# A shifted-window attention block on one core: a second tile for the high and low halves of q and k, an exponential moved ahead of v's evacuation, and the value projection split over two rounds

## The reference, cut to what matters

```python
y   = roll(layernorm(x), (-3, -3))
win = windows_of_7_by_7(y)                    # 2048 windows of 49 tokens
q, k, v = win @ qkv_w.T
attn = softmax(q @ k.T * 8 ** -0.5 + bias + mask)
x   = x + roll(back(attn @ v @ proj_w.T + proj_b), (3, 3))
out = x + gelu(layernorm(x) @ fc1_w.T + fc1_b) @ fc2_w.T + fc2_b
```

## Time and profile before

| what | value |
|---|---|
| median of three runs | 2187.03 us |
| the profiled execution's own time | 2188.17 us |
| its span, first to last instruction | 2186.4 us |
| TensorE matmul busy / weight loads busy | 2115.9 us (97%) / 1670.1 us (76%) |
| VectorE / ScalarE / GpSimd busy | 1681.2 (77%) / 1535.7 (70%) / 1682.9 us (77%) |
| mean granted TensorE clock | 0.996 |

### The profile page before, as it was taken

One profiled execution on the slowest core, in us unless ns is written; L12 is line 12 of the kernel. 1 busy time (PEld: TensorE's weight loads), 2 busy tenths in 40 slices (PEclk: granted clock), 3 DMA queues, 4 the chain that ended last, 5 costly groups with the idle time before them and its releaser, 6 DMA issues.

```text
span 2186.4 us, 147908 instructions
## 1 busy us (share of the span) xinstructions
PE 2115.9 (97%) x62790; PEld 1670.1 (76%) x62790; DVE 1681.2 (77%) x2975; ACT 1535.7 (70%) x2435; POOL 1682.9 (77%) x1689
## 2 busy tenths in 40 slices
PE   6999999999999999999999999999999999999997
PEld 3777777777777777777777777777777777777775
DVE  5778778777877777787777778778777877877774
ACT  4676776776777677677767777776776777677675
POOL 5777777777778777777778777777777777777774
PEclk8999999999999999999999999999999999999999
DMA  4223233232322233333232233333223232333321
GB/s 111 71 75 80 75 77 77 75 78 75 78 76 75 77 77 77 76 76 77 74 78 76 73 77 77 77 77 77 75 75 78 76 75 76 77 75 76 78 69 35
DMA packets 178588, 165.87 MB, mean 76 GB/s; under 512 B 21144, under 2 KB 152458, under 8 KB 178074
## 3 DMA queue, kind: packets, MB, share of 16 engines
q1 hardware_dynamic: 178074, 157.60, 28.5%
HBM read 28.99 MB, written 25.77 MB: 25 GB/s over the span
## 4 chain that ended last, share of the span: by engine, by line
PE 74%; SPq 9%; issue 5%; DVE 5%; ACT 3%; DMA 3%; POOL 1%; DVEq 0%; ACTq 0%; POOLq 0%
PE O L751 12%; PE S L715 9%; SPq L270 8%; PE ST L731 8%; PE M L824 8%; PE M L759 8%; PE ST L737 7%; PE M L846 7%; PE M L809 5%; PE M L791 4%; PE M L777 3%; DMA kp<-hl 3%; PE M L854 2%; DVE nm L579 2%; PE S L719 2%
## 5 line engine op out<-in xcount | busy, mean ns | idle before, releaser
L324 POOL TENSOR_TENSOR nmd<-diag,nm 121x392 f16<-121x392 f16 x1024 | 852.8, 840 | 452.6 <-DVE nm L579 438.3
L579 DVE TENSOR_REDUCE nm<-S 121x8 f16<-121x392 f32 x1024 | 574.7, 561 | 126.1 <-PE S L715 69.2
L424 ACT ACTIVATE pT<-ST 113x392 f32<-113x392 f32 x1024 | 481.9, 496 | 246.2 <-PE ST L737 241.3
L751 PEld LDWEIGHTS O<-vx,pT 113*49 113x49 f32 x16384 | 546.9, 126 | 45.6 <-issue 5.2
L751 PE MATMUL O<-vx,pT 113*49 113x18 f32 x16384 | 521.7, 196 | 3.9 <-issue 3.8
L715 PE MATMUL S<-kp,qp 128*49 128x49 f16 x16384 | 396.9, 186 | 20.6 <-issue 7.4
L731 PE MATMUL ST<-qp,kp 128*49 128x49 f16 x16384 | 389.7, 185 | 16.6 <-ACT pT L424 11.2
L715 PEld LDWEIGHTS S<-kp,qp 128*49 128x49 f16 x16384 | 313.2, 103 | 111.0 <-issue 63.6
L737 PE MATMUL ST<-nmd,shiftw 121*49 121x392 f16 x2048 | 349.1, 336 | 0.3 <-POOL nmd L324 0.2
L731 PEld LDWEIGHTS ST<-qp,kp 128*49 128x49 f16 x16384 | 317.9, 103 | 37.3 <-ACT pT L424 16.9
L405 ACT ACTIVATE hl<-M 128x784 f16<-128x784 f32 x128 | 105.4, 823 | 331.5 <-DMA kp<-hl 173.8
(11 more groups left out here) (90 smaller groups left out, 3258.9 us busy)
## 6 DMA issues: line engine op xcount, KB each, us to landing
qp<-hl SPq DMA_DIRECT2D x1024, 49.0 KB
kp<-hl SPq DMA_DIRECT2D x1024, 49.0 KB
xin<-in_x SPq DMA_DIRECT2D x256, 98.0 KB
out<-res SPq DMA_DIRECT2D x256, 98.0 KB
kp<-in_c_keys SPq DMA_DIRECT2D x4, 588.0 KB, 7.2
weights<-in_c_weights SPq DMA_DIRECT2D x1, 448.0 KB, 3.8
bias_t<-spread SPq DMA_DIRECT2D x2, 73.5 KB, 2.2
shiftw<-in_c_shift SPq DMA_DIRECT2D x1, 139.0 KB
```

What stands on the lines that cost most here:

```text
L324: nc.gpsimd.tensor_tensor(nmd[j % LAG][:], diag[:], nm[j % LAG][:].unsqueeze(2).broadcast_to([RM, 2 * 4, N]), ALU.mult).then_inc(s_nmd, 1)
L424: nc.scalar.activation(pT[j % LAG][:].rearrange("k w h q -> k (w h q)"), ST[0:R, j % 2, 0:HK], ACT.Exp).then_inc(s_e, 1)
L579: V.tensor_reduce(nm[j % LAG][:], S[0:RM, 0:HK].rearrange("q (h n) -> q h n", n=N), AX_X, ALU.max, negate=True).then_inc(s_nm, 1)
L751: mm = MM(O[W0 * w:W0 * w + N, (4 * p + hp) * VC:(4 * p + hp + 1) * VC], pT[j % LAG][:, w, hp, :], vx[r % RING][:, window + 2 * w, hp, :], ...
```

## The change

The change has three parts.

1. There are two `hl` tiles in place of one; unit u uses tile u mod 2. `high_parts` of unit u therefore waits for the DMAs of unit u - 2 in place of those of unit u - 1.
2. On ScalarE, in round 1, exp 7 stands ahead of `place_v` in place of behind it.
3. `project_v` is cut into two halves of 16 matmuls, one in round 1 and one in round 2, each after the transposed scores of that round. Only the second half signals `place_v`.

```diff
-        hl = sb("hl", [128, 2, 2, 2, T // 2], F16)
+        hl = [sb(f"hl{n}", [128, 2, 2, 2, T // 2], F16) for n in range(2)]
...
-                        part = hl[C * qk:C * qk + C, s, b].rearrange("m a t -> m (a t)")
+                        part = hl[r % 2][C * qk:C * qk + C, s, b].rearrange("m a t -> m (a t)")
...
             def high_parts(u, r):
                 act.wait_ge(s_qk, u + 1)
-                if later(u):
+                if later(u, 2):
                     for b in range(2):
-                        act.wait_ge(s_q[(r + 1) % 2][b], 64 * u + 64 - 64 * ((r + 1) % 2))
-                nc.scalar.activation(hl[:, 0].rearrange("m b a t -> m a b t"),
+                        act.wait_ge(s_q[r % 2][b], 64 * u - 64 * (r % 2))
+                nc.scalar.activation(hl[r % 2][:, 0].rearrange("m b a t -> m a b t"),
...
-                    if k == 1 and on_chip(a):
-                        place_v(a, m + 1)
                     u, j = at_unit(i, k, 2)
                     if on_chip(u):
                         exp(u, j)
+                    if k == 1 and on_chip(a):
+                        place_v(a, m + 1)
...
-            def project_v(u):
-                for s in range(8):
+            def project_v(u, half):
+                for s in range(4 * half, 4 * half + 4):
                     for e in range(2):
                         mm = MM(M[W0 * e:W0 * e + N, 2, C * s:C * s + C], yT[:, N * s:N * s + N], wv[:, e, :],
                                 start=True, stop=True, tile_position=(0, W0 * e))
-                mm.then_inc(s_vp, 1)
+                if half == 1:
+                    mm.then_inc(s_vp, 1)
...
-                    if k == 1 and on_chip(a):
-                        project_v(a)
+                    if k in (1, 2) and on_chip(a):
+                        project_v(a, k - 1)
```

More of the change, by code:

```diff
@@ L566, in evac_yT, with low_parts @@
                                 M[:, 1, :].rearrange("c (p w n) -> c p w n", w=2, n=W0)[:, :, :, 0:N], n1w[:, 0:1], n1b[:, 0:1], ALU.mult, ALU.add).then_inc(s_yT, 1)
-            def low_parts(u):
+            def low_parts(u, r):
                 dve.wait_ge(s_hi, u + 1)
-                V.tensor_tensor(hl[:, 1].rearrange("m b a t -> m a b t"),
+                V.tensor_tensor(hl[r % 2][:, 1].rearrange("m b a t -> m a b t"),
                                 M[:, 0:2, 0:HT].rearrange("m a (b t) -> m a b t", b=2),
-                                hl[:, 0].rearrange("m b a t -> m a b t"), ALU.subtract).then_inc(s_lo, 1)
+                                hl[r % 2][:, 0].rearrange("m b a t -> m a b t"), ALU.subtract).then_inc(s_lo, 1)
             def neg_max(u, j):
@@ L655, in body @@
                     if k == 1 and on_chip(a):
-                        low_parts(a)
+                        low_parts(a, m + 1)
                     if k == 2 and on_chip(d):
```

## The result

The changed kernel takes 2246.68 us, the median of four runs (2245.46 to 2249.72). Its ratio to the kernel before is 1.0274 (95% interval 1.026 to 1.0288), so it is 2.7% slower. I had forecast 2219 us, 1.5% slower, and a range that ends at 2245. The direction was right and the size was not. The profiled execution's span is 2245.8 us against 2186.4, which is 59 us more where I had 32. One execution behind this document stands far out: of the eight of E11, a later experiment, one took 10652.71 us for a reason that no trace shows, and without it E11's median would be 2176.97 us in place of 2177.72.

What follows compares the result with a forecast made beforehand. TensorE's list was taken to bound the kernel, with ScalarE's almost without slack in rounds 1 to 4. +68 us for the new wait, -30, -2 and -4 gave +32, or 2219 us for the median, range 2190 to 2245.

Steps and rivals of the forecast that it cites:

- Rival A: Round 4, faster: the late place_v does not reach turn_o, so only gains stay, 2145 us; chance 0.11.
- Rival B: No net change: a delay of 0.29 us at turn_o cancels 36 us of relief, 2183 to 2191 us; chance 0.05.
- rival C: Slower by the whole new wait: DMAs hold the scores, or turn_y delays evacuation and neg_max 5; 2255 us; chance 0.10.
- step 5: Round 4 on TensorE: turn_o starts 0.05 us after the second gelu, 1321.56 in place of 1320.97, 0.59 later.
- the choice of 0.55 us: Delay per pass taken at turn_o, between 0.46 and 0.59 us; over 124 passes 68 us (57 to 73).
- step 4: ScalarE behind place_v: one exp in place of two gives 0.39 us back, so table load and gelus come 0.68 later.
- my own worked value: Delay of turn_o worked out for one clean pass, 0.59 us; with scores 2 earlier it would be 0.46.
- the relief: Hold-ups gone: 30 us for the second hl tile, 2 at the start, 4 for small ones in rounds 2 to 4.

Runs made afterwards that it cites:

- E11: Kernel before with two hl tiles, and project_v cut into two halves that both stand in round 1: 2177.72 us, ratio 0.997.
- E8: Changed kernel with GELU replaced by Identity, so without the two table loads (timing only): 2161.69 us, ratio 0.9901.
- E9: Changed kernel with project_v cut into 24 matmuls in round 1 and 8 in round 2: 2232.38 us, ratio 1.0211.
- E10: Changed kernel with project_v cut into 8 matmuls in round 1 and 24 in round 2: 2269.16 us, ratio 1.0377.
- E6: Changed kernel with turn_o's two waits exchanged, second gelu first and normalise second: 2240.04 us, ratio 1.0249.
- E3: Changed kernel with the one hl tile of before, keeping exp 7 ahead of place_v and the split project_v: 2244.54 us, ratio 1.0271.
- E2: Kernel before with two hl tiles and exp 7 ahead of place_v, project_v whole: 2189.36 us, ratio 1.0012.
- E12: Kernel before with exp 7 ahead of place_v and nothing else: 2190.52 us, ratio 1.0022.
- E5: Kernel before with two hl tiles and turn_o's two waits exchanged, second gelu first and normalise second: 2179.85 us, ratio 0.9976.
- E7: Kernel before with two hl tiles and GELU replaced by Identity, so without the two table loads (timing only): 2172.74 us, ratio 0.9947.

## Why the prediction was wrong in size

**What held.** ScalarE idles ahead of `place_v` (0.60 us in the clean pass, where I had 1316.73 - 1316.16 = 0.57). `place_v` starts 2.64 us behind scores 1, where I had 1316.73 - 1314.10 = 2.63. Scores 2 come 1.52 behind scores 1, as worked out, scores 3 hardly move (2.94 in place of 2.98), the second gelu sets `turn_o`, and no wait of `high_parts` for the DMAs is left. E8 to E10 show that this is the whole cost of the split. Rival A is excluded: `turn_o` was reached. Rival B is too, since the delay at `turn_o` is 0.70 and not 0.29 us. The mechanisms of rival C don't show. TensorE's scores wait once for a DMA out of `hl`, 0.6 us. VectorE's evacuation does wait longer for `turn_y` (28.9 us in place of 5.9), but the scores' waits for `neg_max` didn't grow with it (5.9 us in place of 6.9).

**The step that failed: step 5, and the choice of 0.55 us.** I had the second gelu 0.68 us later in step 4, and the rows give nearly that: it ends 1355.97 - 1348.54 = 7.43 us behind scores 1 where it was 1320.83 - 1314.10 = 6.73, so 0.70 later. Then I let `turn_o` follow it by 0.05 us, the gap between exp 7 and its transposed scores, and so took the 0.14 us in the row of before for 0.09 us of slack. It was no slack. In the kernel before `turn_o` starts 0.14 us behind the second gelu in 78 of the 112 passes, never less, and in 105 of the 112 of the changed one. E6 shows that the 0.09 belongs to the order of the waits. The delay therefore passes in full, 0.70 us. I also went below my own worked value toward a pass in which scores 2 come earlier, and few do (15 of 112). The pass of the fourth kind grew by a little less, 0.64, so the mean clean pass grew by 0.69, from 16.30 to 16.99: 0.55 x 124 = 68 us stood for 0.69 x 124 = 85 us. This is 17 of the 27 us by which I was short.

**The other term: the relief.** I counted 30 us for the second `hl` and 6 us for the start and other hold-ups. The mean pass was 0.32 us above a clean one before. Now a clean pass is about (3 x 16.87 + 17.33) / 4 = 16.99 us, where 17.33 is the usual length of the fourth kind, and the mean is 0.11 above it. That is 0.21 us a pass, or 26 us in all, against 36 forecast, and not for my reason. E1 gives the second tile 11 us by itself, and E3 gives it nothing in the changed kernel. The rest is that the idle stretches at `place_v` and `turn_o` swallow whatever else is late: the changed kernel's 112 passes still hold 60 stops, 27 us together, and are only 13 us longer than clean ones. My count took all of ScalarE's lateness for TensorE's, and gave the single `hl` three quarters of hold-ups of which over half (21 of 36 us) are the stops. The 11 us of E1 are about a third of the 30 that I had read from ScalarE's waits.

The two terms together give 85 - 26 = 59 us, as much as the spans differ by, against the forecast's 68 - 36 = 32.

**A smaller error.** I wrote that the exchange alone costs nothing. With `project_v` whole it costs 0.15 us a clean pass (E2, E12), because exp 7 can't start before shift 7. With the split it starts where I had it, 1.56 us behind scores 1.

**What comes out of it.** Of the versions run with the reference's own function, E1, the second `hl` tile alone, is the fastest: 2174.91 us, 0.9951 of the kernel before (0.9933 to 0.9968). The intervals of E5 and E11, which have the same tile, overlap with it.

## What to carry to other kernels

Follow each engine's list from the signal that a change moves to the next place where the bound engine waits for it. An engine at 70%, as ScalarE was here, can have no slack there, and then a delay arrives whole: 0.13 and 0.22 us at v's signal became 0.14 and 0.22 at `turn_o`. Before a gap between a signal and its waiter is called slack, look for its smallest value over all passes. If many passes share it, it can be the cost of the wait, as it was here: 78 of the 112 passes of the kernel before shared 0.14 us and none had less. And what a side engine waits is not what the bound engine loses: read the bound engine's own waits for it (here 11 us where the side engine had 30), and sort the passes by how late it is.

## What the runs showed of the hardware that I had not expected

At `turn_o` the wait that stands second in the code took longer to pass than the one that stands first. From the end of the second gelu to the first matmul of `turn_o` it was 0.14 us where that wait was second (105 of the 112 passes of the changed kernel) and 0.05 to 0.06 us where it was first (101 of the 112 of E6). From the end of `normalise` it was 0.05 to 0.10 us where that wait was first (E7) and 0.15 us where it was second (E5).

In these traces the wait written second is an instruction of its own, of 51 ns, and the line of the wait written first (L797 in the changed kernel) has none. This is the row of L799, the wait for the gelu, in the changed kernel:

```profile
L799 PEldq EVENT_SEMAPHORE  x126: 51/51/51, 90.7 to 2222.6; - x126
```

In each of the 112 passes it starts 0.04 us after the second gelu's end, and in 105 of them the first weight load of `turn_o` starts 0.08 us after it. In the clean pass of above the gelu ends at 1355.97 and that weight load starts at 1356.08:

```profile
1356.08 0.20 PEld L759 LDWEIGHTS M<-weights,on 113*128 113x128 f32 x2 [0.41 <-issue]
```

TensorE's stops without a named wait go with the loading of instructions, a coincidence in time that every trace shows and no run tests. Each stop within a run of matmuls, 34 to 60 of them in the 112 passes of a kernel and 16 to 34 us together, ends 1.13 to 1.84 us behind the end of an instruction-loading packet (the row q8 above, 496 packets in each trace). These stops are most of what separates the mean pass of E1 from its clean one.
